# Graph attention and mixture of experts on one core: the edge loop's expansion in three bf16 parts at register addresses, comparisons on VectorE, node scale on ScalarE

## The reference, cut to what matters

```python
h = (layernorm(x) @ W.T).reshape(n, 8, 32)
alpha = sum_d(h[src] * a_src) + sum_d(h[dst] * a_dst)
enc = relu(edge_attr @ edge_W.T + edge_b).reshape(-1, 8, 32)
alpha = alpha + sum_d(enc * h[dst])
alpha = where(alpha >= 0, alpha, 0.2 * alpha)
ex = exp(alpha - segment_max(alpha, dst)[dst])
attn = ex / segment_sum(ex, dst)[dst]
x = x + segment_sum(h[src] * attn[..., None], dst) + bias
x = x + moe_ffn(layernorm(x))       # top 2 of 8 experts, 256 -> 1024 -> 256, gelu
```

## Time and profile before

| | us |
|---|---|
| median of three runs | 2126.27 |
| profiled execution, its own time | 2128.02 |
| its span, first to last instruction | 2126.0 |
| `edges`, first VectorE instruction to the rendezvous | 81.3 to 1211.0 |
| `attend` and `route` | 1211 to 1346 |
| `experts` | 1346 to 2126 |

### The profile page before, as it was taken

The page is one execution under the profiler, slowest core; times in us unless marked ns, Lnnn a source line. Parts: engine busy times, 40 slices in busy tenths (PEclk is TensorE's granted clock), DMA queues, the critical chain, the costliest instruction groups (busy, mean ns, idle before and its releaser), DMA issues. The chain is left out here.

```text
span 2126.0 us, 41064 instructions
## 1 busy us (share of the span) xinstructions
PE 2009.7 (95%) x11612; PEld 1585.9 (75%) x11612; DVE 1515.8 (71%) x3458; ACT 1352.4 (64%) x3892; POOL 1181.9 (56%) x1125
## 2 busy tenths in 40 slices
PE   7799999999999999999999676899999999999997
PEld 6566666766666666666666434899999999999996
DVE  7289999999999999999999897544444444444442
ACT  4698888988988988988988565433333333333332
POOL 1377777776776766666666000355555555555553
PEclk9899999999999999999999887999999999999998
DMA  9766565555555555555554688222222222222221
GB/s 252 227 194 175 170 186 175 172 179 165 169 176 163 167 170 163 158 168 160 157 165 143 230 267 190 46 39 36 38 39 36 38 38 36 38 38 36 38 38 23
DMA packets 160559, 270.94 MB, mean 127 GB/s; under 512 B 36239, under 2 KB 114864, under 8 KB 160211
## 3 DMA queue, kind: packets, MB, share of 16 engines
q0 software_dynamic: 61920, 139.45, 27.6%
q1 hardware_dynamic: 89706, 121.22, 18.6%
q10 hardware_dynamic: 8712, 7.65, 1.1%
HBM read 231.06 MB, written 37.17 MB: 126 GB/s over the span
## 5 line engine op out<-in xcount | busy, mean ns | idle before, releaser
L679 POOL DMA_INDIRECT arena<-h_tab,src x784 | 759.6, 969 | 375.6 <-issue 211.8
L1687 ACT ACTIVATE arena<-psum,arena 128x128 f32<-128x128 f32 x840 | 240.1, 368 | 518.2 <-PE psum L1637 518.2
L881 PE MATMUL psum<-arena 128*128 128x256 f32 x1760 | 479.1, 395 | 9.9 <-DVE arena L973 8.0
L902 PE MATMUL psum<-arena 128*128 128x264 f32 x1760 | 475.0, 393 | 2.5 <-DVE arena L996 2.4
L1637 PEld LDWEIGHTS psum<-arena 128*128 128x128 f32 x3360 | 392.9, 192 | 7.5 <-issue 2.2
L902 PEld LDWEIGHTS psum<-arena 128*128 128x128 f32 x1760 | 320.4, 190 | 100.3 <-issue 50.8
L1637 PE MATMUL psum<-arena 128*128 128x128 f32 x3360 | 393.4, 276 | 1.8 <-DVE arena L1709 1.8
L881 PEld LDWEIGHTS psum<-arena 128*128 128x128 f32 x1760 | 318.8, 191 | 98.2 <-issue 42.5
L1653 PE MATMUL psum<-arena 128*128 x1680 | 379.8, 379 | 0.0
L1599 POOL DMA_INDIRECT out_rows<-arena,src x105 | 208.3, 1984 | 247.2 <-DVE arena L1722 244.2
L1653 PEld LDWEIGHTS psum<-arena 128*128 128x128 f32 x1680 | 311.1, 190 | 38.0
(11 more groups left out here) (233 smaller groups left out, 1917.9 us busy)
## 6 DMA issues: line engine op xcount, KB each, us to landing
arena<-rel_list SPq DMA_DIRECT2D x110, 512.0 KB
arena<-in_W SPq DMA_DIRECT2D x16, 1024.0 KB, 12.3
arena<-h_tab,src POOLq DMA_INDIRECT x784
arena<-ea_slots SPq DMA_DIRECT2D x440, 27.0 KB
arena<-in_x SPq DMA_DIRECT2D x12, 896.0 KB, 8.5
h_tab<-arena SPq DMA_DIRECT2D x6, 952.0 KB, 7.9
out_rows<-arena SPq DMA_DIRECT2D x5, 896.0 KB, 5.4
xn<-arena ACTq DMA_DIRECT2D x5, 896.0 KB, 6.9
```

The lines of the kernel that those rows point to most:

```text
L679: pool.indirect_dma_start(rows[:, (p % RING * U + k) * TW:(p % RING * U + k + 1) * TW], None, d.h_tab[:, :], bass.IndirectOffsetOnAxis(ap= ...
L881: last = nc.tensor.matmul(ps[:, HDT + x, y * UE:(y + 1) * UE], hj[:, (s // 2 * 2 + y) % HJ, x * P:(x + 1) * P], oht[:, half % OT, (u + y) ...
L902: last = nc.tensor.matmul(ps[:, AGG + a % 2, 0:HS], oh[:, a % OH, k, :], msg[:, a % MSG, k, :], start=(k == 0), stop=(k == U - 1))
L1687: last = nc.scalar.activation(hT[:, b, h * P:(h + 1) * P], ps[:, UP + 2 * b + half, h % 4 * P:(h % 4 + 1) * P], ACT.Gelu, bias=b1_now[:, b ...
```

## The change

1. The rows of all nodes stay on chip as three bf16 parts whose sum is the f32 value (`PARTS_AT`); the part q of tile j is 256 bf16 values. In `prepare`, POOL splits groups 0 to 5 (cast, subtract, cast, subtract, 128x1792 each), from three staging buffers in place of `h_all`; VectorE splits the last group in steps 2 to 5 of `edges`. ScalarE may overwrite a staging buffer only after POOL has read it.
2. The expansion is three bf16 matmuls in place of one f32 matmul, read at an address that TensorE computes from a register; the one-hot matrix and its list are bf16. `node_rows` and the ring `hj` are gone. TensorE loads the eight tile numbers of a chunk into registers.
3. All comparisons are on VectorE.
4. `fall` and `node_scale` are on ScalarE.
5. The accumulator lies over parts that have been used. Its tiles are cleared two at a time by ScalarE, four times a chunk, ahead of the sums.
6. Some expert weights are loaded at other places: five half rows of W1 at the end of `edges` in place of all eight experts', three experts of W2 and the rest of W1's second half at the start of `attend`, the rest of W2 between the groups of `attend`, seven halves of W1 in `route` in place of six experts of W2.

```diff
+            for i in range(GROUPS - 1):
+                h, rest, first, second, third = parts_of(c, i)
+                pool.wait_ge(h_copied, (i + 1) * GT + 2)
+                nc.gpsimd.tensor_copy(first, h).then_inc(cast, 1)
+                pool.wait_ge(cast, 4 * i + 1)
+                nc.gpsimd.tensor_tensor(rest, h, first, ALU.subtract).then_inc(cast, 1)
+                pool.wait_ge(cast, 4 * i + 2)
+                nc.gpsimd.tensor_copy(second, rest).then_inc(cast, 1)
+                pool.wait_ge(cast, 4 * i + 3)
+                nc.gpsimd.tensor_tensor(third, rest, second, ALU.subtract).then_inc(cast, 1)
+                pool.wait_ge(cast, 4 * i + 4)
...
                 if k == 0:
                     act.wait_ge(rs_made, i + 1)
+                    if i >= 3:
+                        act.wait_ge(rows_stored[i - 3], 32)
+                        act.wait_ge(cast, 4 * (i - 3) + 2)
...
-            def clear_sums(k):
+            def clear_ahead(j, k):
...
+                two = acc[:, ds((j + 2 * k + 1) * ST, 2 * ST)].rearrange("p (b n) -> p b n", b=2)[:, :, 0:HS]
+                nc.scalar.activation(two, c.ones[:, 0:1].unsqueeze(2).to_broadcast([P, 2, HS]), ACT.Copy, scale=0.0).then_inc(cleared, 1)
...
             def factor(ch):
+                before = c_fwd[:, 1 - ch % 2, 2 * CT - 1:2 * CT]
+                act.wait_ge(chain_scanned, 2 * ch + 2)
+                if ch:
+                    act.wait_ge(diag_made, ch)
+                nc.scalar.activation(fall, before, ACT.Relu, bias=c_top[:, 0:1], scale=-1.0).then_inc(fall_made, 1)
                 act.wait_ge(fall_made, ch + 1)
-                nc.scalar.activation(fall, fall, ACT.Exp).then_inc(factor_made, 1)
+                nc.scalar.activation(fall, fall, ACT.Exp, scale=-1.0).then_inc(factor_made, 1)
...
+            def node_scale(ch):
+                act.wait_ge(factored, ch + 1)
+                act.wait_ge(first_kept, 2 * ch + 2)
+                if ch > 1:
+                    act.wait_ge(rescaled, ch - 1)
+                nc.scalar.activation(scale, ps[:, SM, 0:H], ACT.Identity, scale=first[:, ch % 4:ch % 4 + 1], bias=others[:, ch % 4:ch % 4 + 1]).then_inc(scale_made, 1)
...
                 for y in range(2):
-                    last = nc.tensor.matmul(ps[:, HDT + x, y * UE:(y + 1) * UE], hj[:, (s // 2 * 2 + y) % HJ, x * P:(x + 1) * P],
-                                            oht[:, half % OT, (u + y) * UE:(u + y + 1) * UE], start=True, stop=True)
+                    j = js[(s // 2 * 2 + y) % CS]
+                    for q in range(PARTS):
+                        last = nc.tensor.matmul(ps[:, HDT + x, y * UE:(y + 1) * UE], parts[:, ds(j * (PARTS * IN) + (q * IN + x * P), P)],
+                                                oht[:, half % OT, (u + y) * UE:(u + y + 1) * UE], start=(q == 0), stop=(q == PARTS - 1))
...
+                    if t % CS == CS - 1 and t + 1 < SLOTS:
+                        js = load_words(nc, c.slots[0:1, t + 1:t + 1 + CS], mybir.EngineType.PE, 0, J - 1)
...
-                if t % CS in AHEAD_OF and SELECTED * 2 <= t + AHEAD_OF[t % CS] < SLOTS and not by_scalar((t + AHEAD_OF[t % CS]) // 2):
+                if t % CS in AHEAD_OF and SELECTED * 2 <= t + AHEAD_OF[t % CS] < SLOTS:
                     select((t + AHEAD_OF[t % CS]) // 2)
```

270 lines of the change are left out of this document (145 added, 125 removed).

## The result

The changed kernel takes 2135.15 us (median of 6 runs, 2132.93 to 2142.14), the kernel before 2126.39 us beside it. The ratio is 1.0039, with a 95% interval of 1.0024 to 1.0054: 8.8 us more, within the half per cent that the prediction calls no change, and 7 us above the top of its range. The profiled execution has a span of 2134.1 us against 2126.0.

A forecast was written before the change was run, and what follows sets the result against it. The prediction took TensorE as the bound of the steady edge loop (2.46 of 2.484 us a step), GpSimd's gathers as the early one. Sum: 2126.3 - 54 (loop) + 22 (casts) = 2094 us; 8-in-10 range 2060 to 2128.

The forecast's parts named there:

- Expansion: Edge loop, TensorE: six bf16 matmuls 0.11 us apart take 0.66 us instead of 0.86, 0.20 us less a step.
- Registers: Edge loop, TensorE's sequencer: register instructions of 0.28 us a step are hidden; word loads between 0 and 0.07, taken as 0.
- rival A: Edge loop: register writes exposed, step 2.56 us, loop 35 us longer, 2183 us in all; chance 0.10.
- Comparisons: Edge loop, VectorE: 80.5 instead of 60 in 161 steps, at 252 to 488 ns each; middle 0 us a step.
- ScalarE below 1.9 us a step: Edge loop: ScalarE's work after losing L744, squares and relus for comparisons, said to cover fall, node scale and spread clearing.
- I cost it at 0: Edge loop, ScalarE: node scale's wait for TensorE's factors, with relu and one-hot behind it, put at 0.
- The new step: Edge loop: TensorE 2.28 and VectorE 2.27 us, so 2.33 us a step, 2% over the larger; bounds 2.25 and 2.42.
- Rival C: Edge loop: VectorE becomes the bound at its old pace, step 2.40 to 2.43 us, total 2105 to 2130; chance 0.20.
- The loop: Edge loop to last sums: 1067 us against 1121 by the same sum before, -54 us; bounds -73 and -24.
- GpSimd's casts: Stage ahead of the edge loop: six groups of 11.3 us delay its start by 22 us; bounds 0 and 38.
- The rest: Last group's split, list reads, moved weight loads from attend on, expert stage: 0, give or take 3 us.

The follow-up runs named there:

- e4: Changed kernel with the expansion matmuls reading a fixed tile's parts, so no register instructions stand between them: 2127.2 us, one run.
- f7: Changed kernel with fall and node scale back on VectorE: 2149.2 us, ratio 1.0098 to the kernel before.
- f14: Changed kernel with weights split early, five groups cast by GpSimd, three message tiles, six encoded-edge tiles, and sums (reduce) behind the aggregation: 2129.3 us, ratio 1.0008.
- g15: Kernel of f14 with ScalarE's copy of the sums issued behind that step's relu instead of ahead of it: 2102.3 us, ratio 0.9879.
- e9: Changed kernel with three message tiles instead of two, one first-expert weight load moved to attend: 2113.7 us, ratio 0.9928.
- e2: Changed kernel with VectorE's five weight-splitting instructions moved ahead of group 4's statistics, before GpSimd's first cast: 2127.9 us, ratio 1.0004.
- e3: Changed kernel with five second-weight loads in attend issued only after the last group's store: 2140.5 us, ratio 1.0062.
- e7: Same kernel as f7 (changed kernel, fall and node scale back on VectorE), at the lower clock: 2568.4 us beside 2515.9 for the kernel before.
- e13: Changed kernel with five second weights issued behind attend's last stores, at the lower clock: last sums to the end 926.3 us; no total given.
- e11: Changed kernel with early weight split, fewer GpSimd casts, three message tiles, late second weights, six encoded-edge tiles, sums behind aggregation; lower clock: 2561.1 us beside 2515.9 before.
- f15: Same kernel as g15 (f14 with ScalarE's copy of the sums behind relu), at the lower clock: 2546.2 us beside 2504.9 for the kernel before.
- f16: Changed kernel with early weight split, fewer GpSimd casts, three message tiles, and four expansion matmuls instead of six; lower clock: 2543.0 us beside 2504.9 before.

## Why the prediction was wrong, step by step

- **Expansion**: right. 0.11 us apart, 0.82 to 0.83 us for the six, and TensorE's own work is 376.26 / 400 · 2.400 = 2.26 us a step where 2.28 was said.
- **Registers**: right within 0.02 us a step (e4); rival A falls.
- **Comparisons**: 362 ns, inside 252 to 488, and 0.18 us a step before and after: the forecast difference of 0. With the fall and the node scale gone VectorE works 2.22 us a step, below the 2.27. Moving those two is worth up to 0.035 us a step (f7).
- **ScalarE below 1.9 us a step**: wrong. It is busy for 347.31 us, 2.08 a step, since clearing alone is 83 x 631 ns = 52.4 us, 0.31 us a step, and the prediction never worked it out. f14 against g15 shows that ScalarE's order is worth 27 us, so "I cost it at 0" rested on too little, though in the changed kernel itself its order cost nothing that a run shows.
- **The new step, "2.33 us, 2% over the larger"**: the term of the sum that failed in the loop. Both engines' work was sized well and the loss between them was not: 2.400 is 6% over the larger. The 2% has no row behind it. In the kernel before TensorE had no gap, and every wait of VectorE's lay beneath it. Shorten the bound engine and VectorE's wait for the aggregation behind `reduce` comes to the surface, 12.2 us grown to 20.3. With that wait taken away (e9) the step is 2.332. That it then meets the forecast 2.33 is in part luck: both engines work 2.22 us a step there, less than the 2.28 and 2.27 of the sum, and the loss between them is still 5%. Rival C named this step, at its lower edge, and half of the reason, waits that TensorE's lead no longer hides; the other half, comparisons at 488 ns, did not come, and its total ended at 2130.
- **The loop, "-54"**: -36.1. A step 0.07 us longer over 280 steps is 19.6 us, about the 18 missing. The pace of gathers, one in 1.25 us instead of 1.274, lasts to about 600 us in e9 where 490 was said, but the early part is not slower for it: from 200 to 400 us there are 41 and 42 products in 100 us where 39 were said.
- **GpSimd's casts, "+22, all on the path"**: prices near (1.68 and 3.5 to 4.1 us for 1.65 and 3.85; a group 10.8 us where VectorE leaves it alone and 12.0 on average in e2, for 11.3), and with the five instructions out of the casts' way it is 24.3 (e2). What failed is "+22 us, all on the path" as the whole cost: VectorE's two-input and fast instructions are held by GpSimd's and others wait behind them, 33.5 us in all, of which the five instructions' place alone is 9.2.
- **The rest, "0, give or take 3"**: +10.7 us in the profiled execution, about 6 to 7 in the five other runs with the same `attend`. "The moved weight loads have all of attend to land" looked at when they must be there, not at what they share the DMA engines with: VectorE's waits for x, 7.4 us where there were 2.0, come from the loads between the groups for 4.6 us (e3), and likely from those at the head of `attend` for the rest. No order of the loads gave the time back, so what the stage would take with fewer bytes is open.

Together 2094 + 11.5 (start) + 18 (loop) + 10.7 (rest) = 2134 us. Three misses of one sign: each a cost that one engine's traffic lays on another, which a sum over the engines' own instructions doesn't contain. The chances had no case in which the casts were as cheap as forecast and the start still late.

## What to carry to other kernels

When a change takes work from the engine that is full, list the waits that lay beneath it, once a chunk too, before adding a small percentage; a further buffer on the one that comes up can be worth more (19.7 us of the loop here) than work removed (8 to 11 us for a third of the expansion). Work given to GpSimd is paid by VectorE too: look for VectorE instructions with two inputs or fast copies in the same stretch, and move those on the path ahead of it. In a list that an engine works through in order, an instruction whose input may be late should stand behind those that others wait for (27 us, f14 against g15).

## What the hardware did that was not expected

- GpSimd's instructions hold VectorE's to their end: casts of 128x256 from 0.28 to 3.46 to 3.66 us, a subtraction of 128x7 values (L134) from 0.17 to 2.27. It goes the other way too: beside VectorE's casts of 2.0 us in steps 2 to 5 single gathers last 2.07 and 2.64 us instead of 0.95.
- The casts are priced differently beside VectorE's work: a cast of 1792 values 1.68 us alone and 2.03 to 2.66 beside it, a subtraction 3.5 to 3.6 and 3.8 to 4.4.
- Where the chip granted TensorE less clock (between 600 and 1000 us a mean of 0.86 of the 2.4 GHz in e7 and e13, 0.88 in e11 and f15, 0.84 in f16, and 1.00 in all other traces) the loops of these five take 1511 to 1522 us, whatever their work: with two parts or three, with two message tiles or three. The kernels of f7 and g15 are 33 us apart in the loop at full clock, and 7 there (e7, f15). And the order turns round: g15's kernel is 1.2% faster than the kernel before at full clock, and 1.6% slower at the lower one (f15); all five are 1.3 to 2.3% slower than the kernel before beside them. Why a mean clock 12 to 16% lower makes the loop 40% longer is open; there is no trace of the kernel before at that clock.
